# The last block of 8 rows goes through layer 0 in the setup, laid out as 4 column groups

## The chip, the cores and the metric

The kernel runs on 1 core of one Trainium2 chip. The metric is the device time in microseconds (us) of one execution. Five engines of the core matter: TensorE (PE in the profile, its weight loads PEld), VectorE (DVE), ScalarE (ACT), GpSimd (POOL) and SyncE (SP), which issues the transfers.

## The reference, cut to what matters

Two layers of a graph network over N = 5000 nodes with F = 128 features. `adj` is a 0/1 matrix of 5000 x 5000 in float32 (100 MB).

```python
def layer0(x, A, h0, y):                      # _L0_gnn_ref
    adj = A * (y @ y.T)                       # keep edges inside a class
    adj = adj / maximum(sum(abs(adj), axis=1), 1e-12)
    return 0.9 * (adj @ x) + 0.1 * h0
def layer1(h, adj, ...):                      # _L1_gnn_ref, adj used twice
    filt = tanh(adj * adj) * (adj > 0)        # top_k of 350 keeps all of it
    h2 = tanh(h @ W_proj + b_proj)
    return relu(filt @ (h2 @ W_gcn) + b_gcn)
x = layernorm(x + layer0(x, adj, h0, y))
x = layernorm(x + layer1(x, adj, adj, ...))
```

## The kernel before, in words

`packed_path` is the path that runs; `general_path` is a fallback that a flag on the device selects and that does not run on these inputs. The 5000 rows are 40 blocks: 39 of 128 rows (block 0 to block 38) and the block `LAST` (39) of 8 rows. Layer 0 and layer 1 each multiply, for every row block, the 0/1 matrix by 40 column blocks; a "product" below is one such matmul.

**Setup.** From the labels y, 25 pairs of matmuls (`gram_words`, L499) make the words of the class mask, 16 columns to a word (`g_words`); ScalarE and VectorE split the features x into a high and a low half in float16 (`high_part`, `low_part`).

**Layer 0 (steps t = 0 to 46, software pipelined).** SyncE loads the rows of block t in two halves of 2688 and 2312 columns (`load_rows`, L328) into two buffers. VectorE casts them to 0/1 in bfloat16 (`cast`, L797). TensorE packs them into 16-bit words, which also turns them (`pack_rows`, L466: 40 small matmuls against `pack`), and ScalarE moves the words from PSUM to `a_words` (`words_of`, L697). VectorE masks them with the class words (`mask`, L907) and unpacks them into float8 (`unpack`, L878, 8 instructions). Two steps later TensorE multiplies them by the features (`multiply`, L530: 21 and 19 products). VectorE and GpSimd normalise, TensorE applies the two weight matrices (L580, L600, L589), and ScalarE and VectorE store the features of layer 1 as `f_parts` (L753, L926). ScalarE also counts the zeros of every half (`count_zeros`, L676), which a check uses.

Block 39 has the same instructions as any other block, on 8 partitions: two casts, two counts, 40 packing matmuls, a mask, and 40 products with 8 columns of weights.

**Layer 1.** The words of layer 0 are unpacked again without the mask, and each block takes 40 products with `f_parts`. The first two blocks begin inside the last steps of layer 0 (`early`, L542), as far as features are ready. After its steps ScalarE measures both feature arrays and the count of ones (L766, L690, L774, a chain of five instructions with accumulators). In VectorE's step 4 of layer 1, `check_sums` (L868) waits for the last of them, and the unpacking of layer 1's block 5 stands behind it on VectorE:

```python
if isinstance(t, int) and t == 4:
    check_sums()
```

Every engine runs its own program in order; the engines are tied by semaphores alone. The order above is written out by hand in the `step` functions of each engine.

Of the kernel before, what the change touches and what calls it, by code (L numbers as in the profile page):

```python
# [36 lines left out]
def packed_path(nc, engines, sem, x, adj, h0, y, w_proj, b_proj, w_gcn, b_gcn, out, flag, s_flag, s_out):  # L37
# [96 lines left out]
    with ExitStack() as ctx:  # L134
# [29 lines left out]
        y_masked = setup[:, NB * 2 * C:2 * NB * 2 * C].rearrange("p (b c) -> p b c", b=NB)  # L164
        TURN = P // (2 * C)
# [67 lines left out]
        s_cleared = sem("s_cleared")  # L233
        s_y = sem("s_y")
# [66 lines left out]

        def gram_bank(g):
# [16 lines left out]
        def copy_gram(copy, eng, g):  # L319
            eng.wait_ge(s_gram, g + 1)  # L320
            t0, b0 = g // GRAMS * PART, g % GRAMS * 2 * TURN
# [5 lines left out]
        def _(sp):  # L327
# [28 lines left out]
            load_rows(0, 0, 0)  # L356
            sp.dma_start(xs[:, 0, :], x[0:P, :]).then_inc(s_in["x0"], 16)
# [103 lines left out]
        def _(pe):  # L461
# [3 lines left out]

            def pack_rows(t, par, m, h):  # L466
                if isinstance(t, int) and t == 0 and h == 0:
                    pe.wait_ge(s_packs, 1)
                pe.wait_ge(s_bits, t * 2 + h + 1)
# [29 lines left out]
            def gram_words(g):  # L499
# [4 lines left out]
                for i in range(2):  # L504
                    k = g % GRAMS * 2 + i
                    mm = pe.matmul(gram_bank(g)[:, i * 256:(i + 1) * 256], y2_t[:, k * P:(k + 1) * P],
                                   y_diag[:, g // GRAMS, :, :].rearrange("p j w -> p (j w)"),
# [6 lines left out]
            def multiply_ready(n, par):  # L514
                pe.wait_ge(s_unpacked, n + 1)
# [14 lines left out]
            def multiply(n, par, m, parts, h):  # L530

                if h == 0:
                    multiply_ready(n, par)
# [8 lines left out]
            def early(t, lo, hi):  # L542

                if lo == 0:
                    multiply_ready(t + NB, t)
# [4 lines left out]
            def step(t, par, pair):  # L550
# [3 lines left out]
                def products(n, n_par, h):  # L554

                    if valid(n):
# [18 lines left out]
                if valid(t - 5):  # L575
                    m5 = rows_of(t - 5)
                    if isinstance(t, int) and t == 5:
                        pe.wait_ge(s_const, 9)
                    pe.wait_ge(s_xn, t - 4)
# [64 lines left out]
        def _(act):  # L644
# [49 lines left out]
            def step(t, par, pair):  # L694
                odd = (par + 1) % 2

                def words_of(n, par):  # L697

                    act.wait_ge(s_packed, n * 2 + 2)
                    act.activation(at(a_words, n, P).rearrange("p (b w) -> p b w", w=PITCH)[:, :, 0:WORDS + 1],  # L700
                                   words[par][:, 0:NB * PITCH].rearrange("p (b w) -> p b w", w=PITCH)[:, :, 0:WORDS + 1],
                                   ACT.Copy).then_inc(s_words, 1)

                if valid(t - 1) and not (isinstance(t, int) and t <= 1):
                    words_of(t - 1, odd)
                if isinstance(t, int) and t >= 1:
# [16 lines left out]
                if valid(t):  # L723
# [16 lines left out]
                if valid(t):  # L740
# [15 lines left out]
                if isinstance(t, int) and t == NB:  # L756

                    last = a_words[:, :, LAST * PITCH:LAST * PITCH + WORDS]
                    act.wait_ge(s_words, NB)
# [818 lines left out]
```

## Time and profile before

| | us |
|---|---|
| median of 3 runs | 466.32 (466.31 to 466.94) |
| profiled execution | 465.94 |
| its span, from first to last instruction | 464.20 |
| PE busy in the span | 437.5 (94%) |
| DVE busy | 377.7 (81%) |
| ACT busy | 264.1 (57%) |
| POOL busy | 160.2 (35%) |

An engine's busy time is the union of its instructions' times. "Idle before" names the engine or transfer that ended a wait. A matmul's own time includes the run through the array, so the pace of a group is read from the distance between its first and the next group's first start. PEclk, the granted clock, is the share of full speed that TensorE was given in a stretch: 1.00 is 2.4 GHz, 0.50 is 1.2 GHz.

### The profile page before, as it was taken

The page shows a single profiled execution, that of the slowest core. Times are in us where ns is not written, and L with a number is a line of the kernel's source. Part 1 is how long each engine was busy: PE and PEld are TensorE (multiplying, and loading weights), DVE is VectorE, ACT ScalarE, POOL GpSimd, SP SyncE. Part 2 cuts the span into 40 slices and gives each one's busy share as a digit, 9 for nine tenths or more (in the row PEclk, how much of TensorE's full clock was granted, in tenths as well). Part 3 has the DMA queues.
Part 4 walks back from the last instruction along what each step waited for, and adds up shares of the span by engine and source line. Part 5 has one row for each costly group of instructions (what it writes and reads, how often), then busy time and mean ns, then how long its engine had stood idle before and what let it go on. Part 6 is the DMA issues. An engine that isn't in the chain of part 4 may idle for free.

```text
span 464.2 us, 15135 instructions
## 1 busy us (share of the span) xinstructions
PE 437.5 (94%) x5104; PEld 385.5 (83%) x5104; DVE 377.7 (81%) x1359; ACT 264.1 (57%) x357; POOL 160.2 (35%) x310
## 2 busy tenths in 40 slices
PE   3669999999999999999999999989999999999994
PEld 2448898888889888888888887878888888888883
DVE  5988999999999999999999975766666666666663
ACT  4997999999999999999999943900000000000000
POOL 3012543555444555544445541212212212212222
PEclk9987999999999999999999999999999999999998
DMA  8999999999999999999999200000000000000000
GB/s 263 409 412 420 416 408 420 420 406 421 408 416 419 421 423 423 422 421 424 419 422 421 83 2 1 13 11 17 11 17 17 11 17 17 17 11 17 17 11 23
DMA packets 25518, 108.50 MB, mean 234 GB/s; under 512 B 5097, under 2 KB 15490, under 8 KB 15490
## 3 DMA queue, kind: packets, MB, share of 16 engines
q1 hardware_dynamic: 25490, 108.14, 57.6%
q8 instruction: 16, 0.26, 0.2%
q14 instruction: 12, 0.10, 0.1%
HBM read 105.57 MB, written 2.56 MB: 233 GB/s over the span
## 4 chain that ended last, share of the span: by engine, by line
PE 75%; DVE 10%; ACT 5%; issue 5%; DMA 2%; POOL 2%; POOLq 0%; DVEq 0%; ACTq 0%; SPq 0%
PE acc L525 64%; PE words L474 6%; DVE a_bits L803 3%; DMA a_rows<-in_adj_dram 2%; PE feat_acc L589 2%; PE proj_acc L600 2%; ACT count_out L690 2%; DVE turned L892 2%; PE xnt_acc L580 1%; ACT count_out L683 1%; ACT x_parts L669 1%; ACT count_out L774 1%; POOL xs L441 1%; DVE z_high L948 1%; ACT count_out L766 1%
## 5 line engine op out<-in xcount | busy, mean ns | idle before, releaser
L525 PE MATMUL acc<-x_parts,turned 128*128 128x257 f16 (+1 forms) x1600 | 195.9, 277 | 3.1 <-DVE turned L892 1.0
L683 ACT ACTIVATE count_out<-a_rows,ones 128x2688 bf16<-128x2688 f32 (+1 forms) x80 | 190.2, 2377 | 0.5
L525 PEld LDWEIGHTS acc<-x_parts,turned 128*128 128x128 fp8e4 (+1 forms) x1600 | 154.9, 98 | 29.1 <-issue 3.8
L525 PE MATMUL acc<-f_parts,turned 128*128 128x256 f16 (+1 forms) x1560 | 169.5, 271 | 1.3 <-DVE turned L892 1.3
L525 PEld LDWEIGHTS acc<-f_parts,turned 128*128 128x128 fp8e4 (+1 forms) x1560 | 150.5, 98 | 19.2 <-issue 1.6
L803 DVE TENSOR_SCALAR a_bits<-a_rows 128x2688 bf16<-128x2688 f32 (+1 forms) x80 | 116.5, 1457 | 1.9 <-DMA a_rows<-in_adj_dram 1.5
L424 POOL TENSOR_TENSOR var_eps<-mean_var,consts 128x1 f32<-128x1 f32 x80 | 18.6, 232 | 265.8 <-DVE mean_var L1104 138.0
L892 DVE TENSOR_SCALAR turned<-a_words 128x320 uint16 (+1 forms) x305 | 66.5, 232 | 51.2 <-PE acc L525 50.8
L427 POOL TENSOR_TENSOR rstd<-var_eps,consts 128x1 f32<-128x1 f32 x80 | 87.6, 1095 | 6.3
L892 DVE TENSOR_SCALAR turned<-same_class 128x320 uint16<-128x320 uint16 x313 | 71.2, 253 | 0.1
L474 PEld LDWEIGHTS words<-pack,a_bits 128*128 128x128 bf16 (+1 forms) x1600 | 51.5, 97 | 8.7 <-DVE a_bits L803 6.7
L474 PE MATMUL words<-pack,a_bits 128*128 128x9 bf16 (+1 forms) x1600 | 52.0, 167 | 5.5 <-DVE a_bits L803 5.5
L904 DVE TENSOR_SCALAR xn<-z,mean_var,rstd 128x128 f32<-128x128 f32 x79 | 32.5, 411 | 2.6 <-POOL rstd L427 0.8
L413 POOL TENSOR_TENSOR h_part<-h_rows,consts 128x128 f32<-128x128 f32 (+1 forms) x40 | 22.3, 557 | 20.5 <-DMA h_rows<-in_L_gnn_h_dram 20.4
L700 ACT ACTIVATE a_words<-words 128x360 f32 (+1 forms) x40 | 18.9, 473 | 16.3 <-PE words L474 16.1
L441 POOL COPY xs<-xn 128x128 f32 (+2 forms) x40 | 25.8, 646 | 0.5 <-DVE xn L904 0.5
L418 POOL TENSOR_TENSOR xh<-h_part,xs 128x128 f32<-128x128 f32 (+1 forms) x40 | 19.9, 499 | 6.5 <-POOL h_part L413 5.6
L1080 DVE SCALAR_TENSOR_TENSOR low_feat<-acc,consts,bg_all 128x128 f32<-128x128 f32 (+1 forms) x40 | 13.8, 345 | 4.6 <-PE acc L525 4.6
L722 ACT ACTIVATE h_t<-proj_acc,bp_col 128x128 f32<-128x128 f32 (+1 forms) x40 | 14.5, 362 | 4.6 <-PE proj_acc L600 3.1
L589 PE MATMUL feat_acc<-wg,h_t 128*128 128x128 f32 (+1 forms) x80 | 15.6, 277 | 0.8 <-ACT h_t L722 0.6
L739 ACT ACTIVATE xn_t<-xnt_acc 128x128 f32<-128x128 f32 (+1 forms) x40 | 11.0, 274 | 8.2 <-PE xnt_acc L580 8.1
L600 PE MATMUL proj_acc<-xn_t,wp 128*128 128x128 f32 (+1 forms) x80 | 15.4, 274 | 0.2 <-issue 0.2
(114 smaller groups left out, 288.7 us busy)
## 6 DMA issues: line engine op xcount, KB each, us to landing
a_rows<-in_adj_dram SPq DMA_DIRECT2D x39, 1344.0 KB, 7.7
a_rows<-in_adj_dram SPq DMA_DIRECT2D x39, 1156.0 KB, 8.2
out_dram<-xn SPq DMA_DIRECT2D x39, 64.0 KB, 1.5
h_rows<-in_L_gnn_h_dram SPq DMA_DIRECT2D x19, 128.0 KB, 8.0
xs<-in_x_dram SPq DMA_DIRECT2D x3, 640.0 KB, 10.0
xs<-in_x_dram SPq DMA_DIRECT2D x1, 512.0 KB, 9.0
y_nat<-in_L_gnn_y_dram SPq DMA_DIRECT2D x1, 304.0 KB, 3.6
a_rows<-in_adj_dram SPq DMA_DIRECT2D x1, 84.0 KB
```

Of the source, the lines that this page charges most:

```text
L413: pool.tensor_tensor(h0_part[0:m, :], h0_rows[slot][0:m, h0_place(c), :], alpha[0:m, :].to_broadcast([m, F]), ALU.mult).then_inc(s_h0part, 1)
L418: pool.tensor_tensor(xh[par][0:m, :], h0_part[0:m, :], at(xs, n, m), ALU.add)\
L427: pool.tensor_tensor(rstd[par][0:m, :], var_eps[0:m, :], neg_half[0:m, :], ALU.pow)\
L441: pool.tensor_copy(at(xs, t - 4, m), xn[par][0:m, :]).then_inc(s_kept, 1)
L474: mm = pe.matmul(words[par][:, b * PITCH:b * PITCH + WORDS + 1], a_bits[h][0:m, c:c + (P - 1) * d + 1:d], pack[0:m, :], start=True, stop=True)
L525: mm = pe.matmul(acc[par][0:m, low:cols], bits, parts[:, b, low:cols], start=first and b == blocks[0], stop=last and b == blocks[-1])
L589: pe.matmul(feat_acc[0:w6, 0:F], h2_t[:, 0:w6], wg[:, :], start=True, stop=True)\
L600: pe.matmul(proj_acc[:, 0:m5], wp[:, :], xn_t[:, 0:m5], start=True, stop=True)\
L683: act.activation(count_out[0:m, 0:w], a_rows[par][h][0:m, 0:w], ACT.Relu, bias=ones[0:m, 0:1], scale=-HUGE, accum_out=col).then_inc(s_coun ...
L803: dve.tensor_scalar(a_bits[h][0:m, 0:w], a_rows[par][h][0:m, 0:w], 1.0, None, ALU.is_equal).then_inc(s_bits, 1)
L892: up = dve.tensor_scalar(turned_at(n, par)[:, :, bit * WORDS:(bit + 1) * WORDS], source, abs(shift), ONE_PAIR, op, ALU.bitwise_and)
L904: return dve.tensor_scalar(xn[par][0:m, :], z[par][0:m, :], mean_var[par][0:m, 0:1], rstd[par][0:m, :], ALU.subtract, ALU.mult)
```

## The change

Block 39 leaves the steps of layer 0 and gets instructions of its own in the setup. Its columns behind the first 128 are cut into groups of 1280, 1280, 1280 and 1032, and group g lies on partitions 32g to 32g+7 of `last_rows`; the first 128 columns stand beside group 0. So one cast of 1408 elements per partition does what two casts of 2688 and 2312 did, and a packing matmul against the block diagonal `group_pack` makes the words of up to four column blocks: 12 matmuls for 40. The buffers lie in `f_parts`, which layer 0 fills later.

- SyncE: five small transfers ahead of the loads of x. The two loads of block 39 into `a_rows` at the end of the stream stay.
- VectorE: two memsets more, four small copies, `cast_last` between the first and second `low_part`, `unpack_last` (one mask, one unpack) at the end of step 0, `keep_last` (one copy) in step 4. Casts, mask and unpack of block 39 leave steps 39 and 40.
- TensorE: `pack_last` between the two halves of block 0's products, `multiply_last` in three parts of 13, 13 and 14 products in steps 1, 2 and 3, into `xnt_acc`. The packing and products of block 39 leave steps 39 and 41.
- ScalarE: the words of block 39 move to step 1. The two counts of block 39 move from step 39 to behind the last step, ahead of the measures.
- The order of the class words changes to groups 0, 4, 1, 2, 3, since block 39 needs group 4.

```diff
@@ sync
             load_rows(0, 0, 0)
+            sp.wait_ge(s_last_cleared, 1)
+            for g in range(GROUPS):
+                w = min(GROUP_COLS, N - P - g * GROUP_COLS)
+                sp.dma_start(last_rows[g * SPREAD_AT:g * SPREAD_AT + TAIL, 0:w],
+                             adj[FULL * P:N, P + g * GROUP_COLS:P + g * GROUP_COLS + w]).then_inc(s_last_rows, 16)
+            sp.dma_start(last_rows[0:TAIL, GROUP_COLS:LAST_COLS], adj[FULL * P:N, 0:P]).then_inc(s_last_rows, 16)
             sp.dma_start(xs[:, 0, :], x[0:P, :]).then_inc(s_in["x0"], 16)
@@ tensor
+            def pack_last():
+                pe.wait_ge(s_last_bits, 1)
+                pe.wait_ge(s_group_pack, 2)
...
+                for i in range(step):
+                    n = GROUPS if 1 + i + (GROUPS - 1) * step < LAST else GROUPS - 1
+                    c = i // 2 * 2 * P + i % 2
+                    pe.matmul(blocks[:, 1 + i:2 + i + (n - 1) * step:step, :], last_bits[:, c:c + 2 * P - 1:2],
+                              group_pack[:, 0:n, :], start=True, stop=True)
...
+            def multiply_last(lo, hi):
+                if lo == 0:
+                    pe.wait_ge(s_last_unpacked, 1)
...
+                for b in range(lo, hi):
+                    mm = pe.matmul(xnt_acc[0:TAIL, 0:PARTS], last_turned[:, b, :].bitcast(F8)[:, 0:TAIL],
+                                   x_parts[:, b, 0:PARTS], start=b == 0, stop=b == LAST)
...
             def pack_rows(t, par, m, h):
+                if isinstance(t, int) and t == LAST:
+                    return
...
                     products(0, 0, 0)
+                    pack_last()
                     products(0, 0, 1)
...
                     pack_rows(t, par, rows_of(t), 0)
+                if not started and t == 2:
+                    multiply_last(NB // 3, 2 * NB // 3)
...
+                if not started and t == 1:
+                    multiply_last(0, NB // 3)
+                if isinstance(t, int) and t == 3:
+                    multiply_last(2 * NB // 3, NB)
@@ scalar
-                if valid(t):
+                if valid(t) and not (isinstance(t, int) and t == LAST):
                     count_zeros(t, par, pair, 0, rows_of(t))
...
             steps(act, step, LAG, first=FIRST)
+            for h in range(2):
+                count_zeros(LAST, LAST % 2, LAST // 2, h, TAIL)
             act.wait_ge(s_counted, 2 * NB)
@@ vector
+            dve.memset(last_rows, 0.0).then_inc(s_last_cleared, 1)
...
+            for g in range(GROUPS):
+                up = dve.tensor_copy(group_pack[g * SPREAD_AT:g * SPREAD_AT + TAIL, g, :], pack[0:TAIL, :])
+            up.then_inc(s_group_pack, 1)
+            def cast_last():
+                dve.wait_ge(s_last_rows, (GROUPS + 1) * 16)
+                dve.tensor_scalar(last_bits, last_rows, 1.0, None, ALU.is_equal).then_inc(s_last_bits, 1)
...
                     low_part(0)
+                    cast_last()
                     low_part(1)
                     low_part(2)
                     copy_words(8)
                     low_part(3)
+                    unpack_last()
```

How it moves the instructions is shown at three places. The first is TensorE from the products of block 0 (step 1) to the first products of block 1 (step 3). Before (`y_t` is `y2_t`, `words` the packing result, `acc` the products, and L506 the class words):

```order
L525 MATMUL acc<-x_parts,turned 128x257 x40
L474 MATMUL words<-pack,a_bits 128x9 x21
...
L506 MATMUL proj_acc<-y_diag,y_t 128x256 x2
L474 MATMUL words<-pack,a_bits 128x9 x40
L506 MATMUL gram_acc<-y_diag,y_t 128x256 x2
L474 MATMUL words<-pack,a_bits 128x9 x19
L623 MATMUL feat_acc<-bg_row,ones 128x128
L525 MATMUL acc<-x_parts,turned 128x257 x21
```

After, where the stationary operand `f_parts` is the memory that holds `last_bits` (L515 to L519) and `last_turned` (L530):

```order
L598 MATMUL acc<-x_parts,turned 128x257 x21
L515 MATMUL words<-group_pack,f_parts 128x4x9 x8
L515 MATMUL words<-group_pack,f_parts 128x3x9 x2
L518 MATMUL words<-group_pack,f_parts 128x9
L519 MATMUL words<-group_pack,f_parts 128x9
L598 MATMUL acc<-x_parts,turned 128x257 x19
...
L547 MATMUL words<-pack,a_bits 128x9 x19
L530 MATMUL xnt_acc<-x_parts,f_parts 8x257 x13
L547 MATMUL words<-pack,a_bits 128x9 x21
L530 MATMUL xnt_acc<-x_parts,f_parts 8x257 x13
```

Twelve packing matmuls stand between the halves of block 0's products, and two parts of block 39's products stand behind packings of blocks 1 and 2; the third part, 14 products, stands at the end of step 3.

The second place is VectorE in step 0, from the unpacking of block 0 to the first cast of block 1, in the changed kernel (L897 is `cast_last`, L1027 and L1031 are `unpack_last`; the other rows are those of before):

```order
L994 TENSOR_SCALAR turned<-same_class 128x40x8 x8
L932 SCALAR_TENSOR_TENSOR x_parts<-xs,x_parts 128x11x128
L897 TENSOR_SCALAR f_parts<-f_parts 128x1408
L932 SCALAR_TENSOR_TENSOR x_parts<-xs,x_parts 128x10x128 x2
L356 CAST g_words<-gram_acc 128x8x8x8
L932 SCALAR_TENSOR_TENSOR x_parts<-xs,x_parts 128x9x128
L1027 TENSOR_TENSOR same_class<-a_words,g_words 128x320
L1031 TENSOR_SCALAR f_parts<-same_class 128x320
L905 TENSOR_SCALAR a_bits<-a_rows 128x2688
```

Three instructions are new ahead of the first cast of block 1.

The third place is the end of ScalarE's program, from the last tanh to the last measure. Before, followed by after (`h_t` is `h2_t`):

```order
L722 ACTIVATE h_t<-proj_acc,bp_col 128x40
L752 ACTIVATE f_parts<-feat_acc 8x128
L753 ACTIVATE f_parts<-feat_acc 40x128
L766 ACTIVATE count_out,x_sums<-x_parts 128x2560
L690 ACTIVATE count_out,x_sums<-x_parts 128x2560
L690 ACTIVATE count_out,f_sums<-f_parts 128x2560 x2
L774 ACTIVATE count_out,ones_in<-a_words 128x1600
```

```order
L808 ACTIVATE h_t<-proj_acc,bp_col 128x40
L838 ACTIVATE f_parts<-feat_acc 8x128
L839 ACTIVATE f_parts<-feat_acc 40x128
L764 ACTIVATE count_out,zeros_in<-a_rows,ones 8x2688
L764 ACTIVATE count_out,zeros_in<-a_rows,ones 8x2312
L855 ACTIVATE count_out,x_sums<-x_parts 128x2560
L771 ACTIVATE count_out,x_sums<-x_parts 128x2560
L771 ACTIVATE count_out,f_sums<-f_parts 128x2560 x2
L863 ACTIVATE count_out,ones_in<-a_words 128x1600
```

The two counts of block 39 now stand between the last feature and the first measure.

## Rows read from the trace of the kernel before

**Rows 1.** The page, part 4: shares of the chain that ended last

```profile
PE 75%; DVE 10%; ACT 5%; issue 5%; DMA 2%; POOL 2%; POOLq 0%; DVEq 0%; ACTq 0%; SPq 0%
```

**Rows 2.** The chain that ended last, 286 to 310: start us, us, what

```profile
289.25 2.33 ACT count_out L766 x2
...
299.10 3.22 ACT count_out L774 x2
...
302.78 0.37 DVE good L873
...
307.02 3.00 PE acc L525 x26
```

**Rows 3.** Timeline around 300: start, us, engine, line, operation [idle before <-releaser]

```profile
302.34 0.18 DVE L871 TENSOR_SCALAR holds<-x_sums 128x40 f32<-128x40 f32 x1 [2.47 <-ACT count_out L774]
...
307.02 13.21 PE L525 MATMUL acc<-f_parts,turned 128*128 128x256 f16 x121 [1.26 <-DVE turned L892]
```

**Rows 4.** Busy time by stretch: us, PE, PEld, DVE, ACT, POOL, PEclk, DMA share, GB/s

```profile
30.00:36.00 6.00, 3.29 (x65) 2.42 (x63) 4.84 (x13) 5.46 (x7) 0.00 (x0) 0.58 1.01 423
36.00:42.00 6.00, 6.00 (x52) 4.49 (x51) 5.77 (x18) 5.59 (x6) 0.67 (x2) 0.56 1.00 422
42.00:48.00 6.00, 6.00 (x87) 5.36 (x85) 5.42 (x17) 3.92 (x4) 2.15 (x3) 1.00 1.02 420
...
240.00:263.00 23.00, 22.86 (x322) 20.59 (x321) 22.73 (x75) 21.68 (x30) 10.65 (x18) 1.00 0.81 322
```

**Rows 5.** Timeline of PE, 29 to 46

```profile
29.86 0.63 PE L474 MATMUL words<-pack,a_bits 128*128 128x9 bf16 x19 [1.48 <-DVE a_bits L803]
32.01 0.72 PE L474 MATMUL words<-pack,a_bits 128*128 128x9 bf16 x21 [1.52 <-DVE a_bits L803]
...
34.37 0.67 PE L474 MATMUL words<-pack,a_bits 128*128 128x9 bf16 x19 [1.19 <-DVE a_bits L803]
...
35.69 4.70 PE L525 MATMUL acc<-x_parts,turned 128*128 128x257 f16 x21
...
43.81 2.51 PE L525 MATMUL acc<-x_parts,turned 128*128 128x257 f16 x21
```

**Rows 6.** Timeline of DVE in the setup

```profile
16.43 0.32 DVE L915 TENSOR_TENSOR same_class<-a_words,g_words 128x320 uint16<-128x320 uint16 x1
...
24.21 1.55 DVE L803 TENSOR_SCALAR a_bits<-a_rows 128x2688 bf16<-128x2688 f32 x1
27.24 0.69 DVE L322 CAST g_words<-proj_acc 128x512 uint16<-128x512 f32 x1 [1.48 <-PE proj_acc L506]
```

**Rows 7.** Timeline of SP's queue: one small issue

```profile
14.21 0.43 SPq L346 DMA_DIRECT2D h_rows<-in_L_gnn_h_dram  x1
```

**Rows 8.** Timeline of PEld, 265 to 270: the packing of block 39

```profile
265.69 0.59 PEld L474 LDWEIGHTS words<-pack,a_bits 8*128 8x128 bf16 x21 [0.21 <-issue]
...
269.13 0.54 PEld L474 LDWEIGHTS words<-pack,a_bits 8*128 8x128 bf16 x19
```

**Rows 9.** Timeline, 274 to 282: end of layer 0

```profile
274.70 0.16 DVE L938 TENSOR_SCALAR rs<-acc 128x1 f32<-128x1 f32 x1 [0.19 <-PE acc L525]
...
274.82 2.51 PE L525 MATMUL acc<-x_parts,turned 128*8 128x257 f16 x21
...
276.40 1.30 DVE L892 TENSOR_SCALAR turned<-a_words 128x320 uint16<-128x320 uint16 x8
...
277.74 2.29 PE L525 MATMUL acc<-x_parts,turned 128*8 128x257 f16 x19
...
281.67 2.13 PE L525 MATMUL acc<-f_parts,turned 128*128 128x256 f16 x18
```

**Rows 10.** Timeline of ACT, 24 to 30: two counts of one block

```profile
24.07 2.54 ACT L683 ACTIVATE count_out<-a_rows,ones 128x2688 bf16<-128x2688 f32 x1
...
26.79 2.22 ACT L683 ACTIVATE count_out<-a_rows,ones 128x2312 bf16<-128x2312 f32 x1
...
28.92 0.19 ACT L683 ACTIVATION_READ_ACCUMULATOR count_out<-a_rows,ones 128x1 f32 x1
```

More of the change, by code:

```diff
@@ L298, in pair_view, with gram_group, made @@
             return t[:, lo:hi, :].rearrange("p (s e) f -> p s (e f)", e=2)
+        GROUP_ORDER = [0, NB // PART - 1] + list(range(1, NB // PART - 1))
+        def gram_group(g):
+            return GROUP_ORDER[g // GRAMS]
+        def made(n, second):
+            return n if second else n + 1
         def gram_bank(g):
@@ L554, in products @@
                 def products(n, n_par, h):
-                    if valid(n):
+                    if valid(n) and not (isinstance(n, int) and n == LAST):
                         multiply(n, n_par, rows_of(n), x_parts, h)
@@ L739, in step @@
                     act.activation(xn_t[:, 0:m5], xnt_acc[:, 0:m5], ACT.Copy).then_inc(s_xnt_sb, 1)
-                if valid(t):
+                if valid(t) and not (isinstance(t, int) and t == LAST):
                     count_zeros(t, par, pair, 1, rows_of(t))
@@ L876, in check_sums, with unpack @@
                 assert k[0] == CHECKS
-            def unpack(n, par, m, source, lo, hi):
+            def unpack(n, par, m, source, lo, hi, second=False):
                 if isinstance(n, int) and n == NB + 2:
                     if lo == 0:
-                        dve.wait_ge(s_bits, 2 * NB)
-                        dve.wait_ge(s_counted, 2 * NB)
+                        dve.wait_ge(s_bits, 2 * LAST)
+                        dve.wait_ge(s_counted, 2 * LAST)
                 elif lo == 0 and (not isinstance(n, int) or n >= 2):
-                    dve.wait_ge(s_acc, n - 1)
+                    dve.wait_ge(s_acc, made(n - 2, second and not (isinstance(n, int) and n == NB)))
                     if isinstance(n, int) and n == NB:
@@ L933, in normalize_block, with sums @@
                 normalize(n, par, rows_of(n)).then_inc(s_xn, 1)
+            def sums(n, par):
+                return last_sums if isinstance(n, int) and n == LAST else acc[par]
             def row_scale(n, par, m):
-                dve.wait_ge(s_acc, n + 1)
+                if isinstance(n, int) and n == LAST:
+                    dve.wait_ge(s_last_kept, 1)
+                else:
+                    dve.wait_ge(s_acc, n + 1)
                 dve.wait_ge(s_z, n)
-                dve.tensor_scalar(rs[0:m, 0:1], acc[par][0:m, 2 * F:PARTS], 2 * SCALE * L1_EPS,
+                dve.tensor_scalar(rs[0:m, 0:1], sums(n, par)[0:m, 2 * F:PARTS], 2 * SCALE * L1_EPS,
                                   1 / (1 - ALPHA), ALU.max, ALU.mult).then_inc(s_floor, 1)
@@ L1003, in step @@
                     return
-                if valid(t):
+                whole = valid(t) and not (isinstance(t, int) and t == LAST)
+                whole1 = valid(t - 1) and not (isinstance(t, int) and t - 1 == LAST)
+                if whole:
                     cast(t, par, pair, 0)
@@ L1041, in step @@
                     add_low(t - 3, odd, m)
-                if valid(t):
+                if whole:
                     cast(t, par, pair, 1)
@@ L1051, in step @@
                     copy_words_of(t)
+                if isinstance(t, int) and t == 4:
+                    keep_last()
                 begin(NB + 1, 0, 0, BITS)
@@ L1070, in bits @@
                     if valid(t) and (not isinstance(t, int) or t > 2):
[L1071 removed]
+                        unpack(t + NB, par, rows_of(t), words_at(t), lo, hi, True)
                 bits(0, 2)
```

105 lines of the change are left out of this document (83 added, 22 removed).

## The prediction

> **What bounds the kernel now.** I read the chain of waits first. TensorE holds 75% of it, ScalarE only 5% [rows 1], but where that 5% lies decides this change. From 289.25 to 302.3 us the chain does not run over TensorE: it runs through ScalarE's five measuring instructions, then VectorE's check, and comes back to TensorE at 307.02 [rows 2]. The timeline says the same from the other side: VectorE sat idle for 2.47 us until ScalarE's last count ended, ran the check at 302.34, unpacked behind it, and TensorE, out of unpacked bits, waited 1.26 us [rows 3]. So at the seam between the layers ScalarE's tail is the slowest of three, by 1.3 us. Everywhere else the stretches show TensorE full: 6.00 of 6.00 us from 42 to 48, 22.86 of 23 in the last steps of layer 0 [rows 4]. VectorE is as full there, and the transfers at a share of 1.0; so work added to TensorE after some 36 us, or a slip of it, is not won back, while TensorE has 2.7 us idle from 30 to 36 [rows 4], in three waits for casts of 1.48, 1.52 and 1.19 us [rows 5].
>
> **Setup.** VectorE gets the new cast of 1408 elements. A cast of 2688 takes 1.55 us [rows 6], so this one 0.81. Then a mask at 0.32 [rows 6], one unpack at 1.30/8 = 0.16 [rows 9], and four copies on 8 partitions, which have no row; the nearest small one, at 274.70 on one column, takes 0.16 [rows 9], so up to 0.6 and, pipelined, perhaps 0.4. The sum of 1.7 us stands ahead of the casts of block 1. TensorE gets 12 packing matmuls between the halves of block 0's products; 21 of them took 0.67 [rows 5], so 0.4. VectorE's own wait of 1.48 us at 27.24 [rows 6] is for TensorE, which slips with it, so only part is absorbed. The memsets run while VectorE has nothing to do at the start, and I cost them at nothing; uncovered they would be some 0.8 us (1408 elements, priced as the cast). SyncE's five issues at 0.43 [rows 7] put x and the second block's rows 2.2 us later into the queue. The transfers are at full share there [rows 4], so queued data and not the issue sets when rows land; what they add is 0.16 MB, or 0.4 us at 423 GB/s, beside a slip of VectorE that is larger. At most they cost that 0.4.
>
> The products of block 39 are 40 on TensorE. At full clock 21 take 2.51 [rows 5], some 0.112 each from start to start. The first 26 (2.9 us) stand in steps 1 and 2, where the three waits offer 4.2 us [rows 5]: nothing. The last 14 stand at the end of step 3, at about 44 us, with no idle time behind them: 14 x 0.112 = **1.6 us**, which I take for the whole setup. Upwards nothing excludes that the 1.7 + 0.4 us come on top: 3.7. Downwards: TensorE's granted clock is 0.58 and 0.56 from 30 to 42, against 1.00 before and after [rows 4], a mix of 1.2 and 2.4 GHz after the stretch of waits; the first half of block 1's products took 4.70 us there, and 2.51 for block 2 [rows 5]. If the 26 products keep TensorE so busy that the clock stays up, 2.2 us come back: -0.6.
>
> **Layer 0's end.** The packing of block 39, 0.59 + 0.54 [rows 8], leaves TensorE's full queue: **-1.1**. Casts and mask that leave VectorE there cost nothing before, since TensorE was the later one.
>
> Its products, 2.51 + 2.29 less the overlaps, some 4.7 us [rows 9], also go. But they filled TensorE while block 38 was normalised. Count from 274.70, where VectorE takes over the sums of block 38. Before, the first layer 1 product starts at 281.67, 7.0 later [rows 9]. It needs the first unpacking of layer 1, which VectorE does behind block 38's statistics: begun at 276.40, 1.30 long, so done 3.0 later [rows 9]; then a low half of features, a small matmul that waits for it, another one, together some 0.9. I walk to 3.9 instead of 7.0, a gain of 3.1, and lose perhaps 0.3 of it on the round trips to ScalarE of the last blocks: **-2.8** for the last stored feature. Bounds: -4.7 if nothing is exposed, -1.5 if the round trips cost half.
>
> **ScalarE's tail.** The two counts of block 39 ran beside TensorE's products and cost nothing. Now they stand behind the last feature and ahead of the measures. A count's time goes with the columns, not the partitions: two of them took 24.07 to 29.11, **+5.0** [rows 10], and that is known well. The check, the unpacking behind it and TensorE's restart all wait for this tail. So relative to block 38's end the restart moves by -2.8 + 5.0 = +2.2, though TensorE arrives there 2.8 earlier.
>
> **The pause.** TensorE's wait of 1.26 us [rows 3] becomes 1.26 + 5.0 = 6.3 us, whatever the seam gains, because gain and arrival move together. Before, waits of 1.2 to 1.5 us in a row ended with the clock at 1.2 GHz [rows 4, 5], so I take it that 6.3 us do. Coming back cost 4.70 - 2.51 = 2.2 us on the first 21 products [rows 5] and little after: **+2.2**; 0 if the clock holds, some 3.5 if it returns half as late again.
>
> The Trainium skill, "TensorE: Matmul & The Clock Gate", Part 1, has the half clock as the default state that activity releases; that speaks against any change that opens a pause, and the trace agrees with its 0.58 and 0.56 [rows 4]. By its section Terms the penalty is the throttled time x (1 - K/N); for the stretch from 30 to 42, throttled about 10.3 of 12 us by rows 4, that would be 5.2 us in place of 2.2, and the sum +7.9.
>
> **Sum.** +1.6 - 1.1 - 2.8 + 5.0 + 2.2 = **+4.9 us** on the profiled execution of 465.94, so 470.8. That execution is 0.38 below the median of the runs; against the median it is **471.2**. Layer 1 after the restart is TensorE's alone, so nothing of it is won back.
>
> **The rivals.**
> - *Clock holds over the pause.* TensorE pays ScalarE's tail alone: +2.7, so 469.0. For it: the 1.26 us wait did not lower it. Against: the fall within 30 to 36 us, after far shorter waits. 0.17.
> - *A second fall at the seam.* Without block 39's products TensorE has only small matmuls for about 3 us around block 38's end, as sparse as 30 to 36 us. Then the early products run at 1.2 GHz and the last feature is up to 2.2 later: 473.4. 0.13.
> - *The setup slips in full.* VectorE's 1.7 and the 0.4 of packing are not absorbed: 473.3. Nothing but the waits of rows 5 speaks against it. 0.11.
> - *The clock stays down longer after the pause.* The granted clock stood low for some 10.3 of the 12 us from 30 to 42 [rows 4]; with TensorE full for as long, half is lost, 5.2 in place of 2.2: 474.2. Against it: there TensorE waited through the first half, and after the pause it does not. The page's penalty, above, gives the same. 0.06.
> - *Faster: a fuller setup holds the clock.* The 26 products lie where TensorE had fallen to half speed; the first products of block 1 then take 2.5 us instead of 4.7. With -0.6 for the setup, -1.1, the seam's whole 4.7 and no clock loss: -0.6 - 1.1 - 4.7 + 5.0 = -1.4, so 464.9. It decides from the point where setup, seam and clock together give 5.0, ScalarE's price. 0.10.
> - *The tail is not what it seems:* if VectorE reaches the check late anyway, or TensorE has work it can start meanwhile, gains and counts cancel within 0.9 us: 466.3. Against it is the 2.47 us wait of rows 3. 0.07.
>
> **How the numbers follow.** The likeliest, 0.36, gives 471.2; its own bounds run from 469 to 473. A measurement of this kernel can tell some 0.2%, 0.9 us. Faster by more takes the faster rival: 0.10. Within it lies the cancelling case: 0.07. Slower takes the rest, 0.83. The range leaves out little: 465.4 to 475.2, down to the edge of the faster rival, up to a second clock fall with part of the setup slip.
>
> **What would show it.** In the profile after: the counts of block 39 right ahead of L855 on ScalarE, some 5.0 us; VectorE's wait at `check_sums` grown from 2.5 to over 7; one wait of TensorE of about 6 us near 300, and a granted clock under 1 in the stretch after it. Block 38's sums should be ready within 274.7 - 1.1 + 1.6, near 275.2, and the last feature stored some 11.8 us later instead of 14.5. I am wrong if TensorE's wait stays near 1.3 us (then ScalarE's tail was not bound to it), if the clock stays at 1.00 from 30 us on (then the setup gains), or if block 38 ends past 277 (then the setup costs more than its last 14 products).

## The result and the profile after

| | before | changed |
|---|---|---|
| median, us | 466.44 (466.31 to 467.13, 5 runs) | 473.38 (472.95 to 475.27, 5 runs) |
| profiled execution, us | 465.94 | 474.78 |
| its span, us | 464.20 | 472.9 |

The changed kernel takes 1.016 times as long (95% interval 1.0147 to 1.0173): 6.9 us slower by the medians, 8.8 by the two profiled executions, since the profiled one is among the slower of its five. The forecast was 471.2, in a range of 465.4 to 475.2.

The chain of waits, first the page's shares by engine, then its pieces from 276 to 325 us (start, us, what), answers to [rows 1, 2].

```profile
PE 76%; DVE 13%; issue 5%; ACT 3%; POOL 1%; DVEq 0%; POOLq 0%; ACTq 0%
```

```profile
276.65 0.17 DVE rs L1064
...
289.53 0.25 ACT f_parts L839
289.78 2.53 ACT count_out L764 x2
...
294.74 2.44 ACT count_out L855 x2
...
304.72 3.18 ACT count_out L863 x2
...
308.36 0.37 DVE good L975
...
312.53 12.57 PE acc L598 x89
```

The two counts of block 39 (L764) now stand in the chain ahead of the first measure (L855), 289.78 to 294.74. Everything behind them is as in [rows 2], some 5.5 us later: 5.0 by the counts, 0.5 because the last feature is later. The timeline, answering to [rows 3], shows the same as waits:

```profile
307.92 0.18 DVE L973 TENSOR_SCALAR holds<-x_sums 128x40 f32<-128x40 f32 x1 [7.51 <-ACT count_out L863]
...
312.53 7.71 PE L598 MATMUL acc<-f_parts,turned 128*128 128x256 f16 x44 [6.23 <-DVE turned L994]
```

VectorE waits 7.51 us where it waited 2.47, TensorE 6.23 where it waited 1.26. Next the busy times by stretch, columns as in [rows 4]; the two rows in a fence of their own are of PE alone (us, PE, PEclk, DMA share, GB/s).

```profile
30.00:36.00 6.00, 4.39 (x50) 2.59 (x49) 5.97 (x12) 4.75 (x8) 0.31 (x1) 0.63 1.01 421
36.00:42.00 6.00, 6.00 (x68) 4.47 (x65) 4.38 (x16) 4.53 (x5) 0.00 (x0) 0.80 1.01 418
...
276.00:280.00 4.00, 1.74 (x14) 1.25 (x12) 3.06 (x16) 1.35 (x5) 1.22 (x3) 1.00 0.00 0
280.00:284.00 4.00, 3.98 (x22) 2.97 (x23) 3.16 (x17) 0.64 (x2) 1.71 (x4) 0.60 0.00 0
...
312.00:318.00 6.00, 5.47 (x26) 3.94 (x27) 2.92 (x16) 0.00 (x0) 1.79 (x3) 0.50 0.08 22
```

```profile
317.00:318.00 1.00, 1.00 (x6) 0.50 0.00 0
318.00:319.00 1.00, 1.00 (x10) 0.85 0.00 0
```

The same stretch at the seam in the kernel before:

```profile
280.00:284.00 4.00, 3.40 (x29) 2.93 (x28) 3.36 (x16) 1.23 (x5) 1.56 (x4) 1.00 0.00 0
```

The granted clock is low in three places: in the setup, where it was low before too [rows 4]; at the seam, 0.60 from 280 to 284, where before it was 1.00; and behind the pause, 0.50 until some 318.3 us. Ahead of 24 us the column can't be relied on: it shows 1.00 there too, but block 0's first 21 products, at 20.42, take 4.59 us, about as long as 21 products at half clock [rows 5]. TensorE's timeline shows what the first two places do, first one line of the kernel before, then the changed kernel (against [rows 5, 9]):

```profile
26.30 0.67 PE L474 MATMUL words<-pack,a_bits 128*128 128x9 bf16 x21
```

```profile
28.59 0.67 PE L547 MATMUL words<-pack,a_bits 128*128 128x9 bf16 x21 [1.16 <-DVE a_bits L905]
...
32.74 2.96 PE L530 MATMUL xnt_acc<-x_parts,f_parts 128*8 128x257 f16 x13
...
36.28 2.62 PE L530 MATMUL xnt_acc<-x_parts,f_parts 128*8 128x257 f16 x13
...
40.03 2.52 PE L598 MATMUL acc<-x_parts,turned 128*128 128x257 f16 x21
...
45.80 1.73 PE L530 MATMUL xnt_acc<-x_parts,f_parts 128*8 128x257 f16 x14
47.46 2.52 PE L598 MATMUL acc<-x_parts,turned 128*128 128x257 f16 x21
...
280.01 0.46 PE L666 MATMUL feat_acc<-wg,h_t 128*128 128x128 f32 x2 [1.67 <-DVE f_parts L1046]
...
280.53 3.79 PE L598 MATMUL acc<-f_parts,turned 128*128 128x256 f16 x18
```

The first packing of block 1 starts at 28.59; before it started at 26.30. Block 2's first products start at 47.46 instead of 43.81: the setup costs **3.65 us**. The products of block 39 fill the old waits, but at half clock, 2.96 and 2.62 us for 13. At the seam the 18 early products take 3.79 us instead of 2.13. VectorE's timeline shows what it does more in the setup:

```profile
5.69 0.84 DVE L891 COPY group_pack<-pack 8x9 bf16<-8x9 bf16 x4
...
20.27 0.89 DVE L897 TENSOR_SCALAR f_parts<-f_parts 128x1408 bf16<-128x1408 f32 x1
...
26.00 0.32 DVE L1027 TENSOR_TENSOR same_class<-a_words,g_words 128x320 uint16<-128x320 uint16 x1 [0.16 <-ACT a_words L784]
26.36 0.24 DVE L1031 TENSOR_SCALAR f_parts<-same_class 128x320 uint16<-128x320 uint16 x1
26.88 1.56 DVE L905 TENSOR_SCALAR a_bits<-a_rows 128x2688 bf16<-128x2688 f32 x1 [0.28 <-issue]
```

Every one of these is in the chain. The copies delay the first cast of block 0 by 0.73 us (10.89 for 10.16); with cast, mask and unpack the first cast of block 1 is 2.67 later (26.88, before 24.21 [rows 6]) and block 1's first packing 2.29.

Put together, from span to span (+8.7 us):

| place (block 38's sums: VectorE takes them over, L938 before, L1064 after) | predicted | measured |
|---|---|---|
| setup: block 2's first products, 43.81 to 47.46 | +1.6 | +3.65 |
| from there to block 38's sums, 274.70 to 276.65 | -1.1 | -1.7 |
| seam: block 38's sums to the copy of the last feature, 14.30 (274.70 to 289.00) to 12.88 (276.65 to 289.53) | -2.8 | -1.4 |
| from that copy to TensorE's restart, 18.02 to 23.00 | +5.0 | +5.0 |
| from the restart to the end, 157.2 to 160.4 | +2.2 | +3.2 |
| sum | +4.9 | +8.7 |

### The profile page after: what moved, and what is told of

It is laid out like the page before. It is cut to its first block, busy times and chain, and to the rows that moved or that the text cites. A ratio compares the mean times of both kernels' runs of the same rounds, so it can differ in the third digit from the quotient of the medians.

```text
span 472.9 us, 15090 instructions
## 1 busy us (share of the span) xinstructions
PE 440.0 (93%) x5076; PEld 386.0 (82%) x5076; DVE 377.2 (80%) x1365; ACT 264.8 (56%) x357; POOL 160.1 (34%) x310
## 4 chain that ended last, share of the span: by engine, by line
PE 76%; DVE 13%; issue 5%; ACT 3%; POOL 1%; DVEq 0%; POOLq 0%; ACTq 0%
PE acc L598 63%; PE words L547 6%; DVE a_bits L905 4%; DVE turned L994 2%; PE feat_acc L666 2%; ACT count_out L771 2%; PE xnt_acc L530 1%; PE proj_acc L677 1%; PE xnt_acc L657 1%; DVE g_words L356 1%; DVE x_parts L932 1%; ACT count_out L863 1%; DVE z_high L1074 1%; ACT count_out L764 1%; ACT count_out L855 1%
## 5 line engine op out<-in xcount | busy, mean ns | idle before, releaser
L598 PE MATMUL acc<-x_parts,turned 128*128 128x257 f16 x1560 | 188.9, 275 | 3.1 <-DVE turned L994 1.0
L764 ACT ACTIVATE count_out<-a_rows,ones 128x2688 bf16<-128x2688 f32 (+1 forms) x80 | 190.3, 2379 | 0.5
L598 PE MATMUL acc<-f_parts,turned 128*128 128x256 f16 (+1 forms) x1560 | 174.0, 275 | 6.2 <-DVE turned L994 6.2
L598 PEld LDWEIGHTS acc<-f_parts,turned 128*128 128x128 fp8e4 (+1 forms) x1560 | 152.6, 99 | 26.3 <-issue 6.6
L598 PEld LDWEIGHTS acc<-x_parts,turned 128*128 128x128 fp8e4 x1560 | 150.2, 98 | 27.1 <-issue 3.9
L905 DVE TENSOR_SCALAR a_bits<-a_rows 128x2688 bf16<-128x2688 f32 x78 | 113.9, 1461 | 1.0 <-DMA a_rows<-in_adj_dram 0.6
L467 POOL TENSOR_TENSOR rstd<-var_eps,consts 128x1 f32<-128x1 f32 x80 | 86.6, 1083 | 6.3
L547 PEld LDWEIGHTS words<-pack,a_bits 128*128 128x128 bf16 x1560 | 50.2, 97 | 6.6 <-DVE a_bits L905 3.2
L547 PE MATMUL words<-pack,a_bits 128*128 128x9 bf16 x1560 | 50.6, 167 | 3.7 <-DVE a_bits L905 3.7
L481 POOL COPY xs<-xn 128x128 f32 (+2 forms) x40 | 24.6, 614 | 0.4 <-DVE xn L1006 0.4
L764 ACT ACTIVATION_READ_ACCUMULATOR count_out<-a_rows,ones (+2 forms) x80 | 15.5, 194 | 0.0
```

The source lines that it names most:

```text
L467: pool.tensor_tensor(rstd[par][0:m, :], var_eps[0:m, :], neg_half[0:m, :], ALU.pow)\
L481: pool.tensor_copy(at(xs, t - 4, m), xn[par][0:m, :]).then_inc(s_kept, 1)
L547: mm = pe.matmul(words[par][:, b * PITCH:b * PITCH + WORDS + 1], a_bits[h][0:m, c:c + (P - 1) * d + 1:d], pack[0:m, :], start=True, stop=True)
L598: mm = pe.matmul(acc[par][0:m, low:cols], bits, parts[:, b, low:cols], start=first and b == blocks[0], stop=last and b == blocks[-1])
L764: act.activation(count_out[0:m, 0:w], a_rows[par][h][0:m, 0:w], ACT.Relu, bias=ones[0:m, 0:1], scale=-HUGE, accum_out=col).then_inc(s_coun ...
L905: dve.tensor_scalar(a_bits[h][0:m, 0:w], a_rows[par][h][0:m, 0:w], 1.0, None, ALU.is_equal).then_inc(s_bits, 1)
```

## The experiments

Eleven kernels were run, each beside the kernel before on the same chip (466.4 to 466.5 in all of them). "No reader" matmuls below multiply the identity with 512 columns of `y2_t` into a bank that is free there; nothing uses what they write.

### Is it ScalarE's tail? Four kernels

**e1**: the changed kernel, the counts back in step 39.

```diff
-                if valid(t) and not (isinstance(t, int) and t == LAST):
+                if valid(t):
                     count_zeros(t, par, pair, 0, rows_of(t))
...
-            for h in range(2):
-                count_zeros(LAST, LAST % 2, LAST // 2, h, TAIL)
```

> The changed kernel (473.4) with ScalarE's two counts of block 39 put back into step 39, ahead of the last feature's work; the setup and the absence of block 39 at the seam stay as the change has them. Main theory (the counts behind the last feature lengthen ScalarE's tail by 5.0, and the pause this makes in TensorE at layer 1's fourth block costs another 3.2 by the fallen clock): the pause at the restart returns from 6.2 to under 2, the granted clock stays 1.00 from 300 to 330, and the time is 473.4 - 5.0 - 3.2 = 465.2 (464.5 to 467: if the counts cost something in step 39, a part of 5.0 comes back at the seam, where ScalarE has to copy the last feature). Rival A (the setup's slip and the fallen clock at the seam are what the time rests on, the tail has slack): 470 or more. Rival B (the pause goes, the clock falls all the same): 468.4.

Measured: 465.94 (463.75 to 467.65, 12 runs), 0.9982 of before (0.9965 to 0.9999). VectorE's and TensorE's waits are those of before again, and the clock is 1.00 from 300 to 324, as the main theory has it:

```profile
301.79 0.18 DVE L971 TENSOR_SCALAR holds<-x_sums 128x40 f32<-128x40 f32 x1 [2.47 <-ACT count_out L861]
```

```profile
306.40 17.85 PE L598 MATMUL acc<-f_parts,turned 128*128 128x256 f16 x164 [1.19 <-DVE turned L992]
```

**e2**: the kernel before, with the counts alone moved.

```diff
-                if valid(t):
+                if valid(t) and not (isinstance(t, int) and t == LAST):
                     count_zeros(t, par, pair, 0, rows_of(t))
...
             steps(act, step, LAG, first=FIRST)
+            for h in range(2):
+                count_zeros(LAST, LAST % 2, LAST // 2, h, TAIL)
...
-                        dve.wait_ge(s_counted, 2 * NB)
+                        dve.wait_ge(s_counted, 2 * LAST)
```

> The kernel before (466.4) with one part of the change alone: ScalarE's two counts of block 39 behind its steps, and the wait of the third early unpacking eased to the counts of the 39 blocks before it, as the change has it. Main theory: +5.0 in ScalarE's tail, and the pause in TensorE before layer 1's fourth block, 1.3 long before, becomes 6.3 and costs 2 to 3.5 more by the clock: 466.4 + 5.0 + 3.2 = 474.6 (472 to 475). It can come lower by up to 2.5 if the counts had delayed the last feature in step 39 and now don't. Rival A (the tail has slack): 466 to 467. Rival B (the clock holds over the pause): 471.4.

Measured: 474.73 (474.56 to 475.59), 1.0183 of before (1.0158 to 1.0207).

```profile
308.25 0.18 DVE L873 TENSOR_SCALAR holds<-x_sums 128x40 f32<-128x40 f32 x1 [7.48 <-ACT count_out L776]
```

```profile
312.93 12.32 PE L525 MATMUL acc<-f_parts,turned 128*128 128x256 f16 x87 [6.27 <-DVE turned L894]
```

The two waits are those of the changed kernel (7.51 and 6.23), though this kernel has none of its setup and still has block 39 at the seam. Two moved instructions cost 8.2 us (466.49 here for before), more than the whole change; the rest of the change is worth nothing or a little.

**e3** and **e4**: the changed kernel and the one before, with the check later. Nobody but the verdict at the end needs it.

```diff
-                if isinstance(t, int) and t == 4:
+                if isinstance(t, int) and t == FULL:
                     check_sums()
```

> The changed kernel (473.4) with VectorE's check of the measured sums moved from layer 1's step 4 to its step 39; ScalarE's tail keeps its length. Nothing waits for that tail any more until the end. Main theory: TensorE's wait of 6.2 before layer 1's fourth block goes, with it the 3.2 of the fallen clock, and the check's own five operations move to the last steps: 473.4 - 6.2 - 3.2 + 0..1.5 = 464 to 465.5, with the granted clock 1.00 from 300 to 330. Rival A (the setup and the seam make the time): 470 or more. Rival B (the check's operations, about 2 us of VectorE, stand on the path at the end as they now do at the pause): 466.

> The kernel before (466.4) with only VectorE's check of the measured sums moved from layer 1's step 4 to its step 39. Main theory: the kernel before had 1.3 of TensorE's wait there, and VectorE's 2.5 behind it; 466.4 - 1.3 = 465.1 (464.4 to 465.8). Rival (the wait is taken up by VectorE's own lead and comes back within the next steps): no change, 466.4.

Measured: e3 465.05 (462.27 to 466.28, 12 runs), 0.9955 of before (0.9937 to 0.9974); e4 464.79 (464.31 to 465.57), 0.9962 (0.9951 to 0.9974). The tail is as long as ever in e3, the last count ending at 308.4, but TensorE doesn't stop:

```profile
298.05 26.15 PE L598 MATMUL acc<-f_parts,turned 128*128 128x256 f16 x241
```

So it is not the work that ScalarE got that costs, but that VectorE's program stands still for it with the unpacking behind. With that wait gone from both, the change is level with the kernel before, and one thing is new: twelve runs of e4 spread over 1.3 us, twelve of e3 over 4. e4's gain of 1.7 is a little over the 1.26 of the wait.

### What does the clock cost behind the pause?

**e5**: the changed kernel with 27 no-reader matmuls ahead of layer 1's fourth block.

```diff
+                if isinstance(t, int) and t == 5:
+                    for g in (5 * GRAMS - 1, 5 * GRAMS - 2):
+                        pe.wait_ge(*gram_copied(g))
+                    filler(gram_acc, 27)
                 for h in range(2):
                     multiply(t + NB, par, rows_of(t), f_parts, h)
-            steps(pe, step1, 0)
+            steps(pe, step1, 0, first=7)
```

(`filler` issues that many no-reader matmuls; `first=7` writes out TensorE's first seven steps of layer 1 instead of three, so that step 5 can differ.)

> The changed kernel (473.4) with 27 matmuls of 128x512 whose result nobody reads, put into TensorE's queue ahead of layer 1's fourth block, where it waits 6.2 us; at full clock a 512-column one takes some 0.21, so they fill 5.8 of the pause and don't lengthen it. ScalarE's tail stays. Main theory: the restart stays near 312.5, the granted clock is 1.00 in 312 to 318 instead of 0.50, and the 3.2 us of the fall are saved: 470.2 (469.3 to 471). Rival A (what is lost behind the restart is VectorE, which has to catch up, not the clock): no change, 473.4. Rival B (the clock falls though TensorE is busy with these): 473.4 with a granted clock of 0.50.

Measured: 470.6 (469.17 to 472.28), 2.8 less than the changed kernel.

```profile
307.03 5.78 PE L509 MATMUL gram_acc<-y_t,ident_b 128*128 128x512 bf16 x26
...
313.11 17.14 PE L603 MATMUL acc<-f_parts,turned 128*128 128x256 f16 x157 [0.30 <-DVE turned L1003]
```

```profile
312.00:318.00 6.00, 5.70 (x50) 4.61 (x49) 3.85 (x22) 0.00 (x0) 1.98 (x4) 1.00 0.09 25
```

The restart is no earlier (313.11, in the changed kernel 312.53), but the clock is 1.00 and from the restart to the end it takes 157.2 us (span 470.3), exactly as before the change; without these matmuls it took 160.4. The 3.2 us are the clock. The prediction set beside its 2.2 a rule of the Trainium skill, "TensorE: Matmul & The Clock Gate", section Terms: throttled time x (1 - K/N). For the half clock from 312.53 to some 318.3 its estimate is half of 5.8, 2.9 us; the trace agrees within 0.3. The 2.2 that I took from the setup is 1.0 off.

### What does the setup cost, and why does the time spread?

All three kernels stand on e3 (465.05).

**e6** leaves 39 of block 39's 40 products out, and so its sums.

```diff
-                for b in range(lo, hi):
+                for b in range(lo if hi < NB else LAST, hi if hi == NB else lo):
                     mm = pe.matmul(xnt_acc[0:TAIL, 0:PARTS], last_turned[:, b, :].bitcast(F8)[:, 0:TAIL],
-                                   x_parts[:, b, 0:PARTS], start=b == 0, stop=b == LAST)
+                                   x_parts[:, b, 0:PARTS], start=True, stop=True)
```

> The changed kernel with the late check (465.05), with 39 of block 39's 40 products in the setup left out; its packing, cast, mask and unpacking stay. It tells what of the setup's 3.65 us (block 2's first products at 47.46 instead of 43.81) is TensorE's products and what is VectorE's work ahead of block 1's casts. Theory V (VectorE's four small copies 0.73, cast 0.8, mask and unpacking 0.6 aren't absorbed): TensorE's first packing of block 1 stays at some 28.6 where it was 26.3, block 2's first products start near 46.1, the granted clock is low until some 43, and the time is 465.05 - 1.4 = 463.7 (463 to 464.5). Rival, as in the prediction (VectorE's work is absorbed, the products are the price): block 2 starts at 44 and the time is 465.05 - 3.65 = 461.4.

Measured: 462.37 (461.72 to 463.9), between the two.

```profile
28.31 0.67 PE L547 MATMUL words<-pack,a_bits 128*128 128x9 bf16 x21 [1.27 <-DVE a_bits L905]
...
37.58 3.87 PE L598 MATMUL acc<-x_parts,turned 128*128 128x257 f16 x21
...
44.90 2.52 PE L598 MATMUL acc<-x_parts,turned 128*128 128x257 f16 x21
```

The first packing is 2.0 later than in the kernel before (28.31 for 26.30): VectorE's work is not absorbed there, as theory V has it. But block 2 starts at 44.90 and not 46.1; the first products of block 1 take 3.87, in the kernel before 4.70, so the clock came back a little earlier. So of the 3.65, 2.6 went with the 39 products, of which the last 14 are 1.7, and 1.1 stayed, VectorE's work for the most part. The split is one execution against another, and their clocks differ.

**e7** moves the four small copies behind VectorE's copy of the turned y, where it waits anyway.

```diff
-            for g in range(GROUPS):
-                up = dve.tensor_copy(group_pack[g * SPREAD_AT:g * SPREAD_AT + TAIL, g, :], pack[0:TAIL, :])
-            up.then_inc(s_group_pack, 1)
...
             dve.tensor_copy(y2_t[:, 0:TURNED * P], y_turned[0]).then_inc(s_yt_dve, 1)
+            for g in range(GROUPS):
+                up = dve.tensor_copy(group_pack[g * SPREAD_AT:g * SPREAD_AT + TAIL, g, :], pack[0:TAIL, :])
+            up.then_inc(s_group_pack, 1)
```

> The changed kernel with the late check (465.05), with VectorE's four copies of the packing table (0.84 us from 5.69) moved behind its copy of the turned y, where it waits 0.84 for TensorE anyway. Theory V: the first cast of rows begins at 10.2 instead of 10.9, TensorE's first packing of block 1 and block 2's first products come 0.7 earlier, and the time is 464.3 (463.8 to 464.8). Rival (this slip is absorbed by TensorE's wait for casts behind it): no change in block 2's start, 465.05.

Measured: 464.31 (462.14 to 465.51), the number expected, but not by the mechanism:

```profile
10.14 1.56 DVE L900 TENSOR_SCALAR a_bits<-a_rows 128x2688 bf16<-128x2688 f32 x1
...
13.35 1.36 DVE L900 TENSOR_SCALAR a_bits<-a_rows 128x2312 bf16<-128x2312 f32 x1 [0.46 <-DMA a_rows<-in_adj_dram]
```

The first cast is 0.75 earlier, the second waits for its rows, and TensorE's first packing of block 1 starts at 28.55, no earlier than in the changed kernel. The 0.7 between the medians is smaller than either kernel's spread: no gain is shown.

**e8** puts 5 and 6 no-reader matmuls into TensorE's two waits for the casts of block 1.

```diff
+                if not started and t == 1:
+                    pe.wait_ge(*gram_copied(1))
+                    filler(acc[1], 5)
                 if valid(t):
                     pack_rows(t, par, rows_of(t), 0)
...
+                if not started and t == 1:
+                    filler(acc[1], 6)
                 if valid(t):
                     pack_rows(t, par, rows_of(t), 1)
```

> The changed kernel with the late check (465.05), with 5 and 6 matmuls of 128x512 whose result nobody reads in TensorE's two waits for the casts of block 1 (1.16 us at 28.6 and 1.48 at 32.1), some 1.1 and 1.3 us long. Main theory (the clock falls in these waits, and the 13 + 13 products of block 39 behind them take 2.96 and 2.62 instead of 1.45 each because of it): granted clock 1.00 from 24 to 42, both groups near 1.45, block 2's first products some 2.7 earlier, 462.4 (461.5 to 463), and less spread between runs. Rival A (the clock falls all the same): 465 or more. Rival B (the casts and the transfer of the rows come next, so that TensorE only waits longer): under 1 us of gain, 464.3.

Measured: 462.31 (461.27 to 463.5), 0.992 of before (0.9906 to 0.9934).

```profile
32.45 1.61 PE L535 MATMUL xnt_acc<-x_parts,f_parts 128*8 128x257 f16 x13
...
34.65 1.61 PE L535 MATMUL xnt_acc<-x_parts,f_parts 128*8 128x257 f16 x13
...
44.82 2.52 PE L603 MATMUL acc<-x_parts,turned 128*128 128x257 f16 x21
...
278.47 2.13 PE L603 MATMUL acc<-f_parts,turned 128*128 128x256 f16 x18
```

```profile
30.00:36.00 6.00, 5.80 (x74) 3.91 (x74) 5.96 (x11) 4.54 (x8) 0.06 (x1) 1.00 1.01 423
```

The clock is 1.00 from 24 us on, the products take 1.61 for 13, and block 2 starts 2.6 earlier than in the changed kernel, as expected. The six runs still spread over 2.2 us.

The 18 early products at 278.47 show where else the spread comes from. In the profiles of e6, e7 and e8 the clock also held at the seam, without anything done there. Then the 18 early products take 2.13, and the copy of the last feature follows block 38's sums by 11.20 us in all three; in the changed kernel, e1, e3 and e5, where it fell, by 12.7 to 12.9. Over whole runs the granted clock, here and in the setup, goes with the time: in e3 the three runs at 0.994 or 0.995 took 462.3 to 463.1 us, the eight at 0.986 or 0.987 464.1 to 466.3. Why it falls in one execution and not in another these runs don't settle.

### Filling the seam, and the same for the kernel before

**e9** is e8 with 2 and 6 no-reader matmuls in the seam's waits; **e11** is e9 with the copies of e7; **e10** is e4 with 6, 6 and 5 in the three waits of [rows 5]. The seam's part of e9's edit:

```diff
+                if isinstance(t, int) and t in (NB + 1, NB + 2):
+                    for g in (5 * GRAMS - 1, 5 * GRAMS - 2):
+                        pe.wait_ge(*gram_copied(g))
+                    filler(gram_acc, 2 if t == NB + 1 else 6)
                 if valid(t - 6):
                     m6 = rows_of(t - 6)
```

> The kernel of e8 (462.3; its six runs lie between 461.3 and 463.5, and the profiled one, 461.3, shows a granted clock of 1.00 around 280 us, where the changed kernel and e3 show it fallen) with 2 and 6 more matmuls of 128x512 that nobody reads in TensorE's waits of 0.6 and 1.7 us behind block 38's sums. Theory (what is left of the spread is the clock at the seam, which falls in some executions and then makes the 18 early products 3.8 long instead of 2.1): all runs come to 461 to 462, median 461.4, spread under 1.2. Rival A (the spread has another source, the arrival of rows): median 462.3, spread near 2 as before. Rival B (these matmuls delay the last features): 462.8 or more, with the clock at 1.00.

> The kernel before with the late check (464.8), with 6, 6 and 5 matmuls of 128x512 that nobody reads in TensorE's three waits for casts at 29.9, 32.0 and 34.4 us (1.48, 1.52 and 1.19 long). It tells what the change's setup costs and its seam gives once neither kernel's clock falls. Theory: the granted clock is 1.00 from 24 to 42, block 1's first products take 2.5 instead of 4.7, block 2's start near 41.6 instead of 43.81, and the time is 462.6 (462 to 463.2). Rival A (the transfer of the rows comes next: VectorE waited 1.28 us for it at 36.2): block 2 starts past 42.8, 463.8 or more. Rival B (the clock falls all the same): 464.8.

> The kernel of e9 with VectorE's four small copies moved behind its copy of the turned y as in e7. In e7 the first cast began 0.75 earlier, but the second one waited 0.46 for rows, and later work waited for ScalarE, so that TensorE's packing of block 1 came no earlier. Theory (the rows' arrival and ScalarE's words are next): within 0.4 of e9, 461.0 to 461.4. Rival (the slip of 0.73 is TensorE's in full once its clock holds): e9 less 0.7, 460.7.

Measured: e9 461.89 (461.59 to 462.85, 4 runs), 0.9907 of before (0.9892 to 0.9922), the lowest median of all, 0.5 above its theory's; e11 462.43 (462.33 to 462.57, 5 runs); e10 464.99 (464.49 to 465.07), where its theory had 462.6. In the profiles of e9 and e11 the clock is 1.00 at the seam and the last feature comes 11.2 us behind block 38's sums, so these matmuls delay nothing. But e9's median is within e8's spread, and e11 met neither of its theories: it is no faster than e9. e10 shows why a held clock wins nothing in the setup of the kernel before:

```profile
35.39 2.52 PE L530 MATMUL acc<-x_parts,turned 128*128 128x257 f16 x21
...
41.77 2.51 PE L530 MATMUL acc<-x_parts,turned 128*128 128x257 f16 x21 [0.42 <-DVE turned L902]
...
48.33 2.51 PE L530 MATMUL acc<-x_parts,turned 128*128 128x257 f16 x21 [0.42 <-DVE turned L902]
```

```profile
48.88 1.56 DVE L813 TENSOR_SCALAR a_bits<-a_rows 128x2688 bf16<-128x2688 f32 x1 [0.69 <-DMA a_rows<-in_adj_dram]
```

The clock held, and block 2 started 2.0 earlier than in the kernel before, yet block 38's sums came at 275.12 (before 274.70, e4 275.40). TensorE now waits for VectorE's unpacking, VectorE for rows, and the lead is gone by 71 us: the packing that starts at 70.67 in the kernel before starts at 71.00 in e10. In e6, e8, e9 and e11 too, with block 2 at 44.8 to 45.5, block 38's sums lie between 274.6 and 275.1 in no order of their starts. So with the clock held in both kernels the changed setup still starts block 2 some 3 us later (41.77 in e10, 44.82 in e8), and nothing of that is left at block 38's sums. No profiled execution has them before 274.56; that the transfers, at a share of 1.0, set this floor is argued from these waits and was not isolated.

## Why the prediction was right, and where its sizes were off

Right in its sign and its main mechanism: ScalarE's tail binds, the two counts lengthen it by 5.0, and TensorE pays for that and for the clock. e1, e2 and e3 show it from three sides: put back, alone, and with the wait removed. All three marks that were named for it (counts ahead of L855, VectorE's wait over 7, one TensorE wait near 6 with a low clock behind) are there. The rivals "the tail is not what it seems" and "clock holds over the pause" are out, and so is the faster one: the setup's clock fell as before. Of the terms:

- **Counts, +5.0**: measured 5.0. **Pause, 6.3**: measured 6.23.
- **Clock behind the pause, +2.2**: measured 3.2 (e5), near its upper bound of 3.5. The step that was off took the price from the setup's first 21 products; behind the pause TensorE was full, and at half clock for 5.8 us.
- **Setup, +1.6**: measured 3.65, at the upper bound, as in the rival "the setup slips in full" (0.11). "Only part is absorbed" of VectorE's slip, and "nothing" for the first 26 products, were wrong steps: VectorE's work, 2.67 us late at the first cast of block 1 for the 1.7 forecast, arrived at the first packing nearly in full (2.0 in e6, 2.29 in the changed kernel), and the 26 products ran at the half clock of the very waits they fill (2.96 and 2.62 for 13, with the clock held 1.61). The text named the sign of that: block 38's sums past 277 would say that the setup costs more than 14 products. They came at 276.65, 1.5 past the 275.2 given there, so that mark was set too far out.
- **Packing, -1.1**: from block 2's start to block 38's sums 1.7 were won. The stretch takes 229.0 to 230.0 us in the nine profiles with the changed setup, 230.9 to 233.4 in the four without. The packing of block 38's first half, the last that both kernels have, starts at 262.83 for 259.45. So 3.38 of the setup's 3.65 us are still there 215 us later, as the prediction has it (a slip is not won back), and 1.4 of the 1.7 are won behind this point, where block 39's packing stood. That it is 1.4 and not 1.1 stays open.
- **Seam, -2.8**: measured -1.4, and -3.1 wherever the clock held (11.20 for 14.30). The walk was right (the first early product at 280.53 is 3.9 us behind block 38's sums, as walked); what it left out is the rival "a second fall at the seam" (0.13), which came true on top of the main case in the profiled execution: 1.66 us on 18 products (3.79 for 2.13). That this rival's 473.4 is the measured median is luck: its other terms are those of the forecast, and setup and clock alone are some 3 us above them.

Together these are 3.8 of the 3.9 us by which the profiled execution exceeds its 470.8. The median, 473.38, lies 1.4 below that execution; a seam with the clock held would bring 1.7, but no profile shows such a run of the changed kernel.

With the check moved out of the way and the clock held, the rest of the change does pay: 461.9 in e9 against 465.0 in e10, the 3.1 us of the seam. Without that care the new work's price in the setup and the gain at the seam about cancel (e1, and e3 against e4); what made the kernel slower was the place where block 39's counts were left.

## What to carry to other kernels

When work is moved, ask of every piece that stays behind who is last in line for it: two counts that cost nothing beside a full TensorE cost 8 us as the tail of a chain that another engine waits for in the middle of its program. A check that only the end needs belongs at the end. And where the rest waits for TensorE, price a pause in it as itself plus the half clock behind it, and work put into a gap at half clock where the gap is one that lowers it.

## What was not expected of the hardware

- The clock behind a pause can be held by matmuls that nobody reads: 27 of 512 columns in the 6.2 us pause kept it at 1.00 and gave 2.8 us, 11 in two waits of the setup 2.7 us by the medians of e3 and e8.
- At the seam, with the same instructions, the clock fell in four profiled executions and held in three, a difference of 1.5 to 1.7 us each. The changed kernel and its variants up to e8 spread over 2 to 4 us, the kernel before over 1 to 3; with setup and seam filled, e9 and e11 spread over 1.3 and 0.2 (4 and 5 runs).
- A lead of 2.0 us in TensorE's setup (e10) was gone by 71 us, while 3.38 of a slip of 3.65 were still there at 259 us: here, with TensorE busy for 98 of the 100 us from 100 to 200, VectorE for 99 and the transfers at a share of 1.01, a slip is kept and a lead is not.
